# First edge sort of a two-layer GNN + transformer kernel: one-hot products summed in PSUM in place of indirect scatters through DRAM, and the second sort's slots worked out during the message passing

## The reference

```python
def _L0_gnn_ref(input, edge_index, edge_vals, weight, bias):
    support = jnp.matmul(input, weight)
    dst, src = (edge_index[0], edge_index[1])
    messages = support[src] * edge_vals[:, None]
    output = jax.ops.segment_sum(messages, dst, num_segments=input.shape[0])
    return output + bias
...
edge_index = jnp.stack([src, dst])
x = x + _L0_gnn_ref(_layernorm(x, axis=-1), edge_index, edge_weight, L0_gnn_weight, L0_gnn_bias)
```

## Time and profile before

| what | value |
|---|---|
| time, median of 3 runs | 3426.34 us (3425.01 to 3428.97) |
| profiled execution, span from first to last instruction | 3425.4 us |
| median less span | 0.9 us |
| PE / DVE / ACT / POOL busy, share of span | 83% / 56% / 43% / 33% |
| POOL: 160 scatters of the first sort (L1432) | 195.7 us busy, 1223 ns each |
| POOL: 166 gathers of the message passing (L1442) | 157.1 us busy, 947 ns each |

### The profile page before, as it was taken

One profiled execution on the slowest core, in us unless ns is written; L12 is line 12 of the kernel. 1 busy time (PEld: TensorE's weight loads), 2 busy tenths in 40 slices (PEclk: granted clock), 3 DMA queues, 4 the chain that ended last, 5 costly groups with the idle time before them and its releaser, 6 DMA issues. The chain is left out here.

```text
span 3425.4 us, 46634 instructions
## 1 busy us (share of the span) xinstructions
PE 2856.4 (83%) x15398; PEld 2001.1 (58%) x15398; DVE 1921.0 (56%) x3873; ACT 1457.3 (43%) x3150; POOL 1119.9 (33%) x1143
## 2 busy tenths in 40 slices
PE   1304879999958994789999798889999999998899
PEld 1101228777646762444444585558777787776687
DVE  8004874677641114479998526653677536776544
ACT  0000003566514542556666435543566435665322
POOL 6777766467013433076665000000000000001210
PEclk9757999999969997889999899989999999999999
DMA  4105776533157993544442264214422044311322
GB/s 113 33 6 142 211 201 154 124 61 70 39 161 247 339 335 112 192 154 139 138 137 83 98 191 91 57 58 139 121 61 61 15 151 109 77 44 42 101 74 85
DMA packets 228769, 407.93 MB, mean 119 GB/s; under 512 B 48706, under 2 KB 146288, under 8 KB 224438
## 3 DMA queue, kind: packets, MB, share of 16 engines
q1 hardware_dynamic: 173222, 268.49, 27.4%
q0 software_dynamic: 54864, 136.39, 14.7%
q10 hardware_dynamic: 448, 0.08, 0.0%
HBM read 318.32 MB, written 90.35 MB: 119 GB/s over the span
## 5 line engine op out<-in xcount | busy, mean ns | idle before, releaser
L904 ACT ACTIVATE at_p<-at_pb,at_max 125x1250 f32<-125x1250 f32 (+4 forms) x320 | 383.8, 1199 | 302.4 <-DVE at_unused L975 273.7
L790 PE MATMUL at_pb<-ident,at_p 125*125 125x125 f32 x2880 | 433.0, 281 | 21.3 <-ACT at_p L904 18.2
L790 PEld LDWEIGHTS at_pb<-ident,at_p 125*125 125x125 f32 x2880 | 390.2, 191 | 83.9 <-ACT at_p L904 22.4
L807 PE MATMUL at_pb<-at_pt,at_v 125*64 125x250 f32 x2880 | 355.3, 383 | 5.2 <-DVE s_t L1008 3.0
L1475 PE MATMUL so_ps<-g_got,g_hot 128*125 128x512 f32 x332 | 177.6, 635 | 210.4 <-DMA g_got<-support,g_edges 177.9
L968 DVE TENSOR_REDUCE at_wide<-at_pb 125x1 f32<-125x1024 f32 x240 | 293.6, 1223 | 21.0 <-PE at_pb L773 2.9
L890 ACT ACTIVATE at_pt<-at_pb 125x500 f32<-125x500 f32 (+1 forms) x448 | 232.8, 520 | 96.2 <-PE at_pb L790 92.3
L712 POOL TENSOR_TENSOR s_t<-s_t,at_all 128x500 f32<-128x500 f32 (+1 forms) x33 | 42.8, 1297 | 654.2 <-DVE s_t L1008 654.0
L807 PEld LDWEIGHTS at_pb<-at_pt,at_v 125*64 125x64 f32 x2880 | 188.4, 137 | 103.9 <-issue 14.5
L750 PE MATMUL at_pb<-at_s,at_shared 128*128 128x500 f32 (+1 forms) x1152 | 230.0, 362 | 22.8 <-ACT at_shared L852 22.8
L1475 PEld LDWEIGHTS so_ps<-g_got,g_hot 128*125 128x125 f32 x332 | 51.7, 189 | 336.3 <-issue 211.2
(11 more groups left out here) (326 smaller groups left out, 5508.6 us busy)
## 6 DMA issues: line engine op xcount, KB each, us to landing
w_ring<-in_L_ffn_w SPq DMA_DIRECT2D x128, 512.0 KB, 12.2
at_shared<-k_parts SPq DMA_DIRECT2D x64, 312.5 KB
ml_w<-in_mlp_w SPq DMA_DIRECT2D x64, 256.0 KB
k_parts<-at_shared SPq DMA_DIRECT2D x64, 250.0 KB, 3.1
q_parts<-at_shared SPq DMA_DIRECT2D x64, 250.0 KB, 3.3
h_edges<-em_both SPq DMA_DIRECT2D x11, 1024.0 KB, 4.1
g_h<-h_edges SPq DMA_DIRECT2D x11, 1024.0 KB, 5.8
at_shared<-q_parts SPq DMA_DIRECT2D x32, 312.5 KB
```

Source lines behind the costliest of these rows:

```text
L790: ins = pe.transpose(pturn[0:TN, g % 2, TN * (t % 4):TN * (t % 4) + TN], p[:, u % 2, TN * t:TN * t + TN], c.ident[0:TN, 0:TN])
L807: ins = pe.matmul(pout[side:side + 64, 0:2 * TN], v[:, t, 2 * j + h, :], p_t[:, q % 2, t, :], start=(t < 2), stop=(t >= keys[u] - 2))
L904: act.activation(p[:, t % 2, 0:w], score[t % 2][0:TN, 0:w], ACT.Exp, bias=neg_max[:, t:t + 1], accum_out=total[:, t:t + 1]).then_inc(exp_d ...
```

## The change

`place_edges` and `FirstLayer` become one stage, `first_layer`, with a class `Slots` that holds the slot arithmetic in pieces. The first sort no longer moves edges through DRAM. For each of the 160 columns DVE writes three arrays: `to_part` (125 x 128: the one-hot of the edge's row), and two rows of `to_tile` (125 x 166 each: the one-hot of its group times a packed number, and times the weight). PE multiplies them and sums all 160 products in one PSUM bank, which then holds for each slot the packed number (sending node * 128 + receiving node's place in its tile) and the weight. DVE takes it apart into `ids`, `near` and `by`; POOL gathers with `ids` straight from SBUF. The second sort's slot arithmetic (`two`) is called from the loop over groups, at i = 16, 30 to 33, 36, 40, 50 to 53, 56, 60 and 64. The normalisation `y` is written by ACT, the bias is added by POOL, x is loaded from ACT's queue, the second sort's rows are packed by POOL, and of ten `project` calls three come before the sort's products and seven between them.

```diff
-        sp.wait_ge(self.sent, 16 * EC)
-        for n, t in enumerate((slice(0, FIRST_EDGES), slice(FIRST_EDGES, NS))):
-            sp.dma_start(self.edges[:, t, :], self.table[:, t, :]).then_inc(self.edges_in[n], 16)
...
-    def gpsimd(self, pool):
-        for t in range(EC):
-            pool.indirect_dma_start(self.table_d, bass.IndirectOffsetOnAxis(ap=self.slots[:, t:t + 1], axis=0),
-                                    self.rows[:, t, :], None).then_inc(self.sent, 16)
...
-        for i in range(NT):
-            dve.tensor_scalar(self.y[:, i, :], acc[:, i, :], mv[:, i, 0:1], root[:, i:i + 1], ALU.subtract, ALU.mult)\
-                .then_inc(self.normed, 1)
-        dve.wait_ge(self.normed, NT)
-        dve.wait_ge(self.bias_in, 16)
-        for i in range(NT):
-            dve.tensor_tensor(acc[:, i, :], acc[:, i, :], self.bias[:, :], ALU.add).then_inc(self.biased, 1)
...
+    def take_counts(self, dve, own, ps, n):
+        _, j, m = self.banks[n]
+        dve.wait_ge(self.counted, n + 1)
+        own.mark(dve.tensor_copy(self.flat[:, j * EC:(j + m) * EC], ps[:, n, 0:m * EC]))
+    def scan(self, dve, own):
+        own.join()
+        own.step(dve.tensor_tensor_scan(self.run[:, :], self.flat[:, :], self.flat[:, :], 0.0, ALU.add, ALU.bypass))
...
+    def ranks(self, dve, own, ps, at, n):
+        _, j, m = self.banks[n]
+        dve.wait_ge(self.counted, len(self.banks) + n + 1)
+        own.mark(dve.tensor_tensor(self.val[:, j:j + m, :].rearrange("p a b -> p (a b)"),
+                                   self.run[0:TN, j * EC:(j + m) * EC], ps[0:TN, at + n, 0:m * EC], ALU.add))
+    def choose(self, dve, own):
+        own.join()
+        for j in range(NT):
+            own.mark(dve.scalar_tensor_tensor(self.val[:, j, :], self.val[:, j, :], self.delta[0:TN, j:j + 1],
+                                              self.oh[:, j, :], ALU.add, ALU.mult))
...
+HOT = 16
+SORT = 12
+PACK = 128
...
+                pool.memset(zero[:, :], 0.0).then_inc(zeroed, 1)
+                pool.wait_ge(loaded, 128)
+                pool.wait_ge(key0_in, 32)
+                pool.tensor_copy(rows_i[:, :, 0], one.key[:, :]).then_inc(packed1, 1)
+                pool.tensor_copy(rows1[:, :, 2], weight[:, :]).then_inc(packed1, 1)
...
+                pool.wait_ge(bias_in, 16)
+                for i in range(NT):
+                    pool.wait_ge(normed, i + 1)
+                    pool.tensor_tensor(acc[:, i, :], acc[:, i, :], bias[:, :], ALU.add).then_inc(biased, 1)
+                for st in stored:
+                    pool.wait_ge(st, 32 * NT // 2)
+                pool.wait_ge(decoded, 1)
+                for i in range(NS):
+                    if i >= RING:
+                        pool.wait_ge(summed, i - RING + 1)
+                    pool.indirect_dma_start(got[:, i % RING, :], None, support_d,
+                                            bass.IndirectOffsetOnAxis(ap=ids[:, i:i + 1], axis=0)).then_inc(got_in[i % RING], 16)
...
+                turn(0)
+                for i in range(FIRST):
+                    project(i)
+                for t in range(EC):
+                    if t % 8 == 7 and FIRST + t // 8 < NT:
+                        project(FIRST + t // 8)
+                    pe.wait_ge(ready, t + 1)
+                    pe.matmul(ps[:, 4, 0:2 * NS], to_part[:, t % SORT, :], to_tile[:, t % SORT, :, :].rearrange("p a b -> p (a b)"),
+                              start=(t == 0), stop=(t == EC - 1)).then_inc(sorted_, 1)
...
+                    if i == 24:
+                        two.count_all(pe, c, ps)
+                    if i == 40:
+                        pe.wait_ge(taken_counts, 1)
+                        two.count_before(pe, c, ps, 0)
...
+                    for to, of in in_two(acc[:, h, :], tiles_of(a["x"])[:, h, :]):
+                        act.dma_start(to, of).then_inc(x_in[n], 16)
...
+                def normal(i):
+                    act.activation(y[:, i, :], acc[:, i, :], ACT.Identity, bias=shift[:, i:i + 1], scale=root[:, i:i + 1])\
+                        .then_inc(normed, 1)
...
+                dve.tensor_scalar(root[:, :], mv[:, :, 1], EPS, None, ALU.add).then_inc(var, 1)
+                one.split(dve, own)
+                dve.wait_ge(rooted, 1)
+                own.step(dve.reciprocal(root[:, :], root[:, :]))
+                dve.scalar_tensor_tensor(shift[:, :], mv[:, :, 0], -1.0, root[:, :], ALU.mult, ALU.mult).then_inc(shifted, 1)
...
+                own.mark(dve.tensor_copy(part[:, :], one.part_i[:, :]))
+                own.mark(dve.tensor_copy(tile[:, :], one.tile_i[:, :]))
+                own.step(dve.tensor_copy(packed[:, :], other[:, :]))
+                own.step(dve.scalar_tensor_tensor(packed[:, :], packed[:, :], float(PACK), local[:, :], ALU.mult, ALU.add))
+                for t in range(EC):
+                    if t >= SORT:
+                        dve.wait_ge(sorted_, t - SORT + 1)
+                    dve.tensor_scalar(to_part[:, t % SORT, :], c.iota[0:TN, 0:TE], part[:, t:t + 1], None, ALU.is_equal)
+                    for n, value in enumerate((packed, weight)):
+                        ins = dve.tensor_scalar(to_tile[:, t % SORT, n, :], c.iota[0:TN, 0:NS], tile[:, t:t + 1], value[:, t:t + 1],
+                                                ALU.is_equal, ALU.mult)
+                    ins.then_inc(ready, 1)
+                tile_owners(dve, own, c, base, off0, base0, NS)
+                dve.wait_ge(sorted_, EC)
+                own.mark(dve.tensor_copy(by[:, :], ps[:, 4, NS:2 * NS]))
+                own.step(dve.tensor_copy(both_i[:, :], ps[:, 4, 0:NS]))
+                own.mark(dve.tensor_scalar(near_i[:, :], both_i[:, :], PACK - 1, None, ALU.bitwise_and))
+                dve.tensor_scalar(ids[:, :], both_i[:, :], PACK.bit_length() - 1, None, ALU.arith_shift_right).then_inc(decoded, 1)
+                own.join()
+                own.step(dve.tensor_copy(near[:, :], near_i[:, :]))
...
+                def second(i):
+                    if i == 16:
+                        dve.wait_ge(key1_in, 32)
+                        dve.wait_ge(packed1, 5)
+                        two.buckets(dve, own, rows1[:, :, 1])
...
+                    if i in (30, 31, 32, 33):
+                        two.take_counts(dve, own, ps, i - 30)
+                        if i == 33:
+                            own.join()
+                            dve.engine_nop().then_inc(taken_counts, 1)
+                    if i == 36:
+                        two.scan(dve, own)
+                    if i == 40:
+                        two.starts(dve, own)
+                    if i in (50, 51, 52, 53):
+                        two.ranks(dve, own, ps, 0, i - 50)
+                    if i == 56:
+                        two.choose(dve, own)
+                    if i == 60:
+                        two.split(dve, own)
+                        dve.scalar_tensor_tensor(slots1[:, :], two.part_i[:, :], float(NS1), two.tile_i[:, :],
+                                                 ALU.mult, ALU.add).then_inc(placed, 1)
+                    if i == 64:
+                        tile_owners(dve, own, c, base, off1, base1, PAIRS)
...
+                    second(i)
...
-                    place("dst", "src", table1, rows1, slots1, off1, NS1, 2 * TE, rest=layer,
-                          owners=((off0, base0, NS), (off1, base1, PAIRS)))
+                first_layer(nc, c, a, support, table1, rows1, slots1, off0, off1, base0, base1, x_sb)
```

More of the change, by code:

```diff
@@ L1373 @@
-HOT = 16
 BY_SHIFT = 20
@@ L2373, in program @@
         make_constants(nc, c)
-        table0, table1 = dram("table0", [128 * NS, ROW]), dram("table1", [128 * NS1, ROW])
-        place = lambda key, other, *to, **more: place_edges(
-            nc, c, a[key], a[other], a["edge_weight"], a["edge_attr_4"], a["edge_attr_8"], *to, **more)
+        table1 = dram("table1", [128 * NS1, ROW])
         support, x1, z2 = (rows(n) for n in ("support", "x1", "z2"))
@@ L2389, in program @@
             with hold() as x_sb:
-                with ExitStack() as first:
-                    rows0 = first.enter_context(nc.sbuf_tensor("rows0", [TN, EC, ROW], F32))
-                    slots0 = first.enter_context(nc.sbuf_tensor("slots0", [TN, EC], I32))
-                    place("src", "dst", table0, rows0, slots0, off0, NS, TE)
-                    layer = FirstLayer(nc, c, first, a["x"], kview(a["L0_gnn_weight"]), a["L0_gnn_bias"], support, table0, base0,
-                                       rows0, slots0, x_sb)
-                    place("dst", "src", table1, rows1, slots1, off1, NS1, 2 * TE, rest=layer,
-                          owners=((off0, base0, NS), (off1, base1, PAIRS)))
+                first_layer(nc, c, a, support, table1, rows1, slots1, off0, off1, base0, base1, x_sb)
                 s_t = s0("s0_t", [128, DC, N])
```

468 lines of the change are left out of this document (209 added, 259 removed).

## The result

The changed kernel takes 3326.43 us (median of 4 runs, 3325.34 to 3329.74), the kernel before 3427.11 beside it: a ratio of 0.9706, 95% interval 0.9694 to 0.9718, 100 us less. The forecast was 3330. The profiled execution has a span of 3327.9 us against 3425.4; it is the longest of the four (spans from 3323.5 us), so the traces are compared by their own marks and the medians by themselves.

What follows compares the result with a forecast made beforehand. POOL was taken as the bound, by scatters until 290 us, then gathers. 3425.4 - 100 (earlier first gather) + 3.5 (loop) = 3328.9 us of span, median 3330; own range 3322 to 3338, with rivals 3310 to 3358.

Steps and rivals of the forecast that it cites:

- first sort product: After normalisation and projections 0 to 2, PE's sort columns start at 54.0 us.
- rest of the program: Everything behind the message loop is unedited and keeps its old length.
- Slots: First sort's slot arithmetic before the statistics: same steps as before plus 1 us for loading key and x together, to 27.4.
- The sort's pace: First sort: PE sets the pace to 112.0 us at 0.56 a column, then DVE at 0.78 for 93 columns, to 184.5.
- rival B: First sort: DVE is faster than PE, so PE binds; 14 us less and some 2 more, 3314; chance 0.12.
- Rival A: First sort: DVE's three instructions do not overlap, 1.0 us a column, 20 us more, 3350; chance 0.15.
- Owners and taking apart: Behind the last sort column: `tile_owners` 4.2 us, copies and shifts 1.1, ending at 189.8; POOL starts at 190.
- The loop: Second sort's DVE work in the message loop: lag beyond 8 to 9 us stops POOL, 3.5 us back.
- Hidden edits: POOL's bias sums and packing (some 20 us), ACT's 0.6 us per tile and PE's counting products (2.85 us) are covered.
- C: Message loop starves: DVE's lumps stop POOL for 14 us instead of 3.5, 3341; chance 0.14.
- D: PE stays at half clock through the first sort; POOL starts at 300 us, 3440; chance 0.02 (given for D and E).
- E: The change does not do what it says: gathers waited for something else than `ids`; chance 0.02 (given for D and E).

Runs made afterwards that it cites:

- keyfirst: Changed kernel with ACT's loads of x held until the first sort's key is in: 3322.93 us, ratio 0.9694.
- twohot: Changed kernel with the weight's one-hot left out from column 12 on (weights wrong): 3308.49 us, ratio 0.9667.
- late: Changed kernel with the second sort's split moved from group 60 to 84 and its `tile_owners` from 64 to 104: 3328.11 us, ratio 0.9710.
- scan5: Changed kernel with five more scans of 1600 columns on DVE in the message loop, results unused: 3338.19 us, ratio 0.9756.
- reduce5: Changed kernel with five more reductions of 1600 elements on DVE in the message loop, results unused: 3327.56 us, ratio 0.9706.
- pieces: Changed kernel with the second sort's scan and subtraction of 1600 columns each cut into eight pieces of 200: 3328.08 us, ratio 0.9717.
- b_half: Kernel before the change with 80 of its 160 first-sort scatters left out: 3309.78 us, ratio 0.967.

## Why the prediction held, by its own steps

| step | forecast | measured |
|---|---|---|
| statistics begin | 27.4 | 27.51 |
| PE's first transpose | 39.5 | 39.44 |
| first sort product | 54.0 | 53.85 |
| column on PE; last projection done | 0.56; 112.0 | 0.56; 111.18 |
| column on DVE; `tile_owners` begins | 0.78; 184.5 | 0.75; 181.69 |
| owners and taking apart, to POOL | 5.3 | 6.0 |
| first gather | 190 | 187.66 |
| given back in the loop | 3.5 | 6.0 |
| rest of the program | as before | 1.2 us less |

*Slots.* Right by luck, by two errors. DVE's first instruction came at 10.01 us, 2.7 later than before, not 1; its steps then took 17.5 us instead of 19.1. keyfirst shows the first: with x asked for behind the key DVE starts at 6.54. The second lies in the kernel before: POOL packed rows beside these steps, and two of DVE's short ones ended only when POOL's copies did. The longer of the two, with the copy beside it:

```profile
19.05 1.17 DVE L1335 TENSOR_SCALAR so_counti<-so_count 128x10 int32<-128x10 f32 x1
```

```profile
18.94 1.25 POOL L1266 COPY rows<-so_a 125x1280 f32<-125x1280 f32 x1
```

In the kernel after the same step takes 0.17 us, since POOL packs only from 27.78 us on. The two steps make 1.5 of the 1.6 us.

*The sort's pace.* Both terms held, and so did the place where they change over: 93 columns of 0.75 us before 181.69 begin at 111.9. twohot shows that PE was waiting behind it, and gives about what rival B would have been: a gather 14.7 us earlier, for which B had 16. Rival A, one-hots that don't overlap, is excluded by starts 0.28 us apart for instructions that last 0.37. The forecast had taken from the Trainium skill, VectorE: DVE Perf Modes, "The DRAIN you can't avoid", that the next instruction waits for an empty pipe. The same paragraph goes on that a next instruction that isn't held starts earlier; the trace shows that second case, 0.09 us earlier.

*Owners and taking apart.* 0.7 us short: POOL's first gather begins 0.9 us after the end of `so_ids` (in the trace at 186.49 for 0.24 us), for which the working had 0.2 (189.8 to 190).

*The loop.* This step failed in its mechanism and in part in its size. It priced DVE's lumps by DVE's lag alone, with POOL waiting for products around steps 44 to 72 for 3.5 us. The lag is there, late removes it, but it was 1.4 us, at steps 73 to 75. 3.5 us came from gathers held while the scan and the subtraction ran, which is shown by scan5 against reduce5. pieces shows that the two are not simply added: while a gather is held POOL asks for nothing, so DVE's lag is partly paid already. Without the holds the waits grew from 1.4 to 5.4 us, and the 3.5 us came back elsewhere; how much of that is due to the 2.2 us that the pieces add to DVE's work wasn't separated. The small rest of the 6.0, some 1 us, is spread over the first gather and steps beside short instructions and wasn't taken apart.

*Hidden edits.* POOL's bias sums were hidden from the gathers, as said, but not free: they hold DVE (below). PE sets the pace there, so it should have cost little; it wasn't tried alone.

*Rivals C, D, E.* C's price was 14 us, the loop gave back 6. D fell: the granted clock was 1.00 from 40 to 188 us. It was 0.74 from 188 to 200, after PE had run out of columns, where the forecast had 1.00; the loop is paced by POOL there. E fell with b_half and the first gather's releaser, `so_ids`.

The span was 1.0 us below the forecast's: the first gather came 2.3 us early, the loop gave back 2.5 more than said, and the rest of the program was 1.2 shorter. That the first two cancel is luck. The 1.2 is no finding: behind the loop the traces of the kernel after and of those built on it take 2912.6 to 2918.2 us. The profiled execution's own time was 3329.74, 1.8 us more than its span. So what a launch takes beside its span is not the forecast's 0.9, which set one execution's span against a median of several; in every execution for which both are known it is 1.7 to 2.4. The median of the four lies 3.3 us below the profiled one, which is scatter between runs. The upper end given for the rivals, 3358, doesn't follow from its own terms: A's 3350 with C's 10.5 us on top is 3360.

## What to carry over

Read the whole stretch in which two engines already run side by side in the kernel before: a transfer's issue that is longer than its neighbours (3.47 against 1.19 us) is a price that can follow the instruction beside it to wherever it is moved. A road that alternates between two engines is shortened by balancing it, not by speeding up one piece: spreading the projections was worth 8.5 us of the first gather and 10 by the medians, most of what all edits together gave (12 by the ratios, 16 by the medians). And a lump taken out of one wait is to be looked for in the next: cutting the scan alone lengthened the loop by 0.7 us, and cutting it with the later lumps drawn apart shortened it by 2.5, in one pair of traces each.

## What the runs showed of the hardware

POOL's indirect transfers are held while DVE runs a long instruction with two operands in SBUF: 3.02 to 4.19 us instead of 0.95 beside a scan of 3.5, 2.37 beside a subtraction of 1.8, at most 0.5 us more beside ten short ones in a row (`choose`, 1.11 in the kernel after, 1.47 in pieces), nothing beside a reduction of 2.9 or beside `x_sb` sums whose second operand is in PSUM. The Trainium skill, SBUF — State Buffer, "Who interferes with whom", has this rule: a DVE instruction with two SBUF inputs contends with a GpSimd instruction that reads SBUF, and one with a single input outside the fast modes does not. The trace agrees. The same section infers that such an instruction doesn't stall the descriptors of a transfer issued by GpSimd; for these indirect transfers the runs show that it does (2.37 us beside a `tensor_tensor` of 1.83, against 0.95).

The other way round, POOL's own sums hold DVE, as its copies did in the kernel before (1.17 us above). The kernel after, timelines of DVE and POOL, where one-hots that otherwise last 0.27 to 0.36 us last 1.3 beside the bias sums:

```profile
39.50 1.32 DVE L1524 TENSOR_SCALAR so_totile<-iota,so_tile,so_packed 125x166 f32<-125x166 f32 x1
40.74 1.31 DVE L1524 TENSOR_SCALAR so_totile<-iota,so_tile,so_w 125x166 f32<-125x166 f32 x1
...
43.19 0.36 DVE L1524 TENSOR_SCALAR so_totile<-iota,so_tile,so_packed 125x166 f32<-125x166 f32 x1
```

```profile
39.45 3.73 POOL L1396 TENSOR_TENSOR x_sb<-x_sb,g_bias 125x512 f32<-125x512 f32 x3 [8.86 <-ACT ln_y L1465]
```

A small load that shares the time with a large one on another queue is late: in the nine traces with x asked for beside it, the key of 160 columns landed at 9.91 to 11.10 us, and at 6.54 to 6.61 in the three with x asked for behind it.
